# First attention of a two-attention transformer kernel: row maxima as undivided products, and the next head's projections, the transposes and the values in other steps

## Reference

```python
H, HD, D = (16, 64, 128)
Q = (x @ Wq.T + bq).reshape(B, N, H, HD)
K = (x @ Wk.T + bk).reshape(B, N, H, HD)
V = (x @ Wv.T + bv).reshape(B, N, H, HD)
scores = jnp.einsum('bnhd,bmhd->bhnm', Q, K)
scores = scores * (SCALE * adaptive_scale)[None, :, None, None] / TEMP
w = jax.nn.softmax(scores, axis=-1)
attn = jnp.einsum('bhnm,bmhd->bnhd', w, V).reshape(B, N, H * HD)
y = x + (attn @ Wo.T + bo)
```

## Time and profile before

| what | value |
| --- | --- |
| median of 3 runs | 2270.84 us (2270.72 to 2274.38) |
| profiled execution, its own time | 2273.7 us |
| span of its profile, first to last instruction | 2271.9 us |
| mean granted TensorE clock | 0.977 of full speed |
| TensorE products busy | 2148.1 us |
| VectorE busy | 1465.8 us |
| ScalarE busy | 1428.5 us |
| GpSimd busy | 1326.7 us |

### The profile page before, as it was taken

The page is one execution under the profiler, slowest core; times in us unless marked ns, Lnnn a source line. Parts: engine busy times, 40 slices in busy tenths (PEclk is TensorE's granted clock), DMA queues, the critical chain, the costliest instruction groups (busy, mean ns, idle before and its releaser), DMA issues.

```text
span 2271.9 us, 50924 instructions
## 1 busy us (share of the span) xinstructions
PE 2148.1 (95%) x21413; PEld 1609.9 (71%) x21413; DVE 1465.8 (65%) x2764; ACT 1428.5 (63%) x1839; POOL 1326.7 (58%) x730
## 2 busy tenths in 40 slices
PE   4999999999999999999999998779999999999998
PEld 3667667667667667667667666557888888878886
DVE  6666666666666666666666665666666666666652
ACT  2677777777777777777777787325554554545553
POOL 4688888788788788788888898122122231221200
PEclk7899999999999999999999999879999999999999
DMA  6211211211211211211211200100000000000000
GB/s 162 57 29 30 57 30 29 58 29 30 57 29 29 57 30 29 57 30 29 57 30 30 57 2 2 47 0 1 1 1 1 1 1 1 1 1 1 1 1 19
DMA packets 46036, 63.33 MB, mean 28 GB/s; under 512 B 9328, under 2 KB 20592, under 8 KB 45552
## 3 DMA queue, kind: packets, MB, share of 16 engines
q1 hardware_dynamic: 45808, 60.08, 11.2%
HBM read 8.67 MB, written 1.05 MB: 4 GB/s over the span
## 4 chain that ended last, share of the span: by engine, by line
PE 83%; DVE 9%; POOL 4%; issue 2%; ACT 1%; SPq 1%; DMA 1%; POOLq 0%; ACTq 0%; DVEq 0%
PE ST L1248 11%; PE ST L1249 9%; PE OO L1191 7%; PE OO L1382 7%; PE RING L1132 5%; PE OO L1192 5%; PE OO L1194 5%; POOL PAB L474 3%; PE OO L1132 3%; PE RING L1335 3%; PE ST L1405 3%; PE ST L1382 3%; PE ST L1409 2%; PE ST L1407 2%; PE RING L1315 2%; PE RING L1119 2%
## 5 line engine op out<-in xcount | busy, mean ns | idle before, releaser
L474 POOL TENSOR_TENSOR PAB<-PR,PAB 128x1024 f16<-128x1024 f32 x512 | 1092.0, 2138 | 228.3 <-ACT PAB L614 205.2
L612 ACT ACTIVATE PR<-ST 128x1024 f32<-128x1024 f32 x512 | 524.7, 1025 | 357.8 <-PE ST L1249 350.6
L826 DVE TENSOR_REDUCE maxes<-RING 128x1 f32<-128x512 f32 x652 | 434.1, 684 | 234.5 <-PE RING L1132 131.6
L614 ACT ACTIVATE PAB<-ST 128x1024 f16<-128x1024 f32 x512 | 521.3, 1018 | 0.0
L1191 PEld LDWEIGHTS OO<-VP,PAB 128*128 128x128 f16 x4096 | 372.5, 96 | 158.1 <-issue 143.5
L1191 PE MATMUL OO<-VP,PAB 128*128 128x66 f16 x4096 | 444.7, 194 | 17.9 <-DVE SHARED L859 13.8
L1248 PE MATMUL ST<-QL,KH 128*128 128x512 f32 x1024 | 448.0, 438 | 0.0
L1192 PE MATMUL OO<-VP,PAB 128*128 128x64 f16 x4096 | 440.7, 194 | 0.0
L1194 PE MATMUL OO<-VP,PAB 128*128 128x66 f16 x4096 | 438.3, 192 | 0.0
L1249 PE MATMUL ST<-QH,KL 128*128 128x512 f32 x1024 | 404.1, 395 | 0.0
L1192 PEld LDWEIGHTS OO<-VP,PAB 128*128 128x128 f16 x4096 | 377.1, 97 | 20.3 <-issue 19.5
(11 more groups left out here) (165 smaller groups left out, 3337.7 us busy)
## 6 DMA issues: line engine op xcount, KB each, us to landing
KH<-HS SPq DMA_DIRECT2D x128, 128.0 KB, 2.3
QL<-HS SPq DMA_DIRECT2D x64, 128.0 KB, 2.4
QL<-F SPq DMA_DIRECT2D x64, 128.0 KB, 2.4
QH<-HS SPq DMA_DIRECT2D x64, 128.0 KB, 2.4
KL<-F SPq DMA_DIRECT2D x64, 128.0 KB, 2.4
X<-in_L_attn_a_x SPq DMA_DIRECT2D x4, 256.0 KB, 3.7
SHARED<-in_rope_cos SPq DMA_DIRECT2D x1, 1024.0 KB, 4.8
SHARED<-in_rope_sin SPq DMA_DIRECT2D x1, 1024.0 KB, 6.9
```

The source lines that it names most:

```text
L474: pool.tensor_tensor(PB[:, s, :], PR[:, step % 2, :], PA[:, s, :], ALU.subtract).then_inc(p_low_ready, 1)
L612: act.activation(PR[:, step % 2, :], ST[step % 2][:, :], ACT.Exp)
L614: act.activation(PA[:, step % SLOTS_A, :], ST[step % 2][:, :], ACT.Exp).then_inc(sa.exps, 1)
L826: dve.reduce_max(maxes[:, i // BLOCKS, i % BLOCKS:i % BLOCKS + 1], bank[:, :], X_AXIS).then_inc(sa.ring_taken, 1)
```

## The change

Each maxima product is now one product over all 128 partitions, QL with KH, where it was a product over 64 partitions: of the first half (QL) for even items and of the second half (QH) for odd ones. Its result has the low part of the queries in it as well. The projections and values of the next head stand in steps 3 and 7 instead of 1 and 4. The transposes stand in step 4 instead of 3; the output product stays in step 5. The lines behind L1132 move up by two.

```diff
-HEAD_STEPS = (1, 4)
+HEAD_STEPS = (3, 7)
...
     if ((ul - 1) % UNITS_A) // BLOCKS == 1 and not (first and ul == 0):
-        items += [("turned",)] if step == 3 else [("output",)] if step == 5 else []
+        items += [("turned",)] if step == 4 else [("output",)] if step == 5 else []
...
                 qt, c = divmod(i, BLOCKS)
                 at = qb * BLK + qt * P
-                row, high = (0, QL) if c % 2 == 0 else (DA, QH)
-                pe.matmul(RING3[item % 3][:, :], high[head % 2][row:row + DA, at:at + P],
-                          KH[head % 2][row:row + DA, c * BLK:(c + 1) * BLK], start=True, stop=True
-                          ).then_inc(sa.ring_put, 1)
+                pe.matmul(RING3[item % 3][:, :], QL[head % 2][:, at:at + P], KH[head % 2][:, c * BLK:(c + 1) * BLK],
+                          start=True, stop=True).then_inc(sa.ring_put, 1)
```

## The result

The changed kernel takes 2237.6 us, the median of five runs (2236.71 to 2238.41), against 2270.72 us for the kernel before on the same chip (2269.56 to 2274.38 over five runs). The ratio is 0.9851 with a 95% interval of 0.9838 to 0.9865: 33.1 us faster, where 33.5 were forecast.

What follows compares the result with a forecast made beforehand. TensorE, busy 95% of the span, was taken to bound the kernel. Gains of 27.4, 15.5 and 1.0 less 10.4 gave 33.5 us, from 2270.84 to 2237 us; own range 2230 to 2246, set range 2226 to 2257.

Steps and rivals of the forecast that it cites:

- (a): First attention's maxima: two full-height products replace each pair, saving 0.055 us in 498 pairs, 27.4 us.
- the gaps stay: Rival: gaps around the maxima come with the ring's banks, so undividing gains nothing; time 2265, chance 0.07.
- a second stream: Rival: undividing leaves both gaps and adds a stream of 0.23 us a pair; time 2380, chance 0.04.
- (b): Projections moved to steps 3 and 7: PV's waits for VectorE in step 2 go, 15.5 us, plus 1.0 in the first block.
- the 29 waits: PV waiting in step 2 for VectorE's product into A2 after a projection: 29 x (2.80 - 2.265) = 15.5 us gained.
- the term for the first block: Very first block: moving a projection out of the low-clock time gains 1.0 us.
- a projection leaves the low clock: Very first block: the projection's two passes, 2.07 us there, take half at twice the clock; 1.0 us gained.
- (c): Transposes moved to step 4, output still in step 5: VectorE's copy stays hidden with 0.9 us to spare, no cost.
- (d): Values moved in block 2: GpSimd's rest delays PV by 0.55 us in 15 heads, 0.26 in 8; 10.4 us lost.
- GpSimd becomes the pace: Rival: GpSimd needs 2.24 us a step beside a working VectorE, reducing the gain to 15; time 2256, chance 0.12.
- does not grow: Step 6: the row product's wait for VectorE's end of the maxima would not grow, first maximum ready 0.1 us earlier.
- 2.50 for step 6: Step 6 of block 2, with its row product, was taken as 2.50 us long, losing some 0.07.

Runs made afterwards that it cites:

- the moves with the earlier rest: Kernel before with projections, values and transposes moved, maxima still divided, and values taken one step sooner on ScalarE and GpSimd: 2258.45 us, ratio 0.9933.
- the change with the earlier rest: Changed kernel with the items of the values taken one step sooner on ScalarE and GpSimd: 2227.1 us, ratio 0.9802 to the kernel before.
- the moves alone: Changed kernel with the half-height maxima products of before, so only projections, values and transposes are moved: 2268.91 us, ratio 0.9985 to the kernel before.
- the third experiment: Changed kernel with GpSimd's rest of the values, and ScalarE's part, taken one step sooner: 2227.1 us against 2272.68 for the kernel before.
- the first experiment: Kernel before with undivided maxima and no other part of the change: 2243.47 us against 2272.68, ratio 0.9872.
- the second experiment: Changed kernel with divided maxima, only the steps of projections, values and transposes moved: 2268.91 us against 2272.68 for the kernel before.
- the version with both edits: Changed kernel with values taken one step sooner on ScalarE and GpSimd, and without L831: 2219.27 us, ratio 0.976 to the kernel before.

## Why the prediction was right, point by point

**(a) Undivided maxima: right.** The pair was priced at 0.52 and two undivided products at 0.46, by the gaps behind score products. After, the gaps are 0.24, 0.22 and 0.24, and a step is 2.21. The nearest measurement is between the moves with the earlier rest and the change with the earlier rest, where no PV waits for the rest of the values: 1304.6 - 1276.1 = 28.5 us beside 27.4. It is not free of the meeting: L831 takes 0.17 in nearly all steps 6 of the first and 0.27 to 0.29 in half of those of the second. The two rivals on this step fall: "the gaps stay" (they closed) and "a second stream" (it came, 0.22 in the kernel after, but the 0.29 that went from the gaps is more). The doubled speed that this last rival rests on did not carry over to a single pair among full-height products: both products together take 0.46 undivided and 0.52 divided. The prediction also read the gaps of 0.33 and 0.43 as the cost of changing the mode. They are not shown to be that, since the gap between two half-height products in turn, 0.34, is as long as the two at the change of height.

**(b) Projections in steps 3 and 7: the price of the 29 waits right, the term for the first block not.** Kernel before to the moves with the earlier rest is 1320.3 - 1304.6 = 15.7, beside 15.5. All 29 waits went. The first block was priced at 1.0; it takes 20.2 instead of 22.7 from its first score product to block 1, 2.5 less, of which 1.0 is lost because the loop starts that much later (63.55 instead of 62.54; the start of the first maxima varies by 1.9 us among the profiles here, and what they wait for is a DMA). TensorE's clock rises to its higher level sooner. The window from 65 to 70 us in the kernel after, to be read beside 0.50 of full speed (1.2 GHz of 2.4) in the earlier trace rows:

```profile
65.00:70.00 5.00, 4.23 (x23) 2.90 (x22) 3.64 (x6) 4.08 (x5) 2.49 (x2) 0.94 0.00 0
```

But the projections don't bring this. With the undivided maxima alone they stand in step 1 as before, and the window shows 1.00 and the block takes 18.7, the shortest of all. In the moves with the earlier rest they stand in steps 3 and 7, and the window shows 0.50 and the block takes 22.9. Over all kernels here this block lasts 18.7 to 20.2 in the five with undivided maxima and 20.5 to 24.6 in the five with half-height ones. So the step of the prediction that failed here is "a projection leaves the low clock": as far as these runs show, what was gained goes with the form of the maxima, whose pairs at the low level the prediction counted as nothing. Why the clock rises earlier with them stays open. The size is uncertain, since the two groups are only 0.3 apart: the moves alone and the moves with the earlier rest have the same work in this block and take 21.4 and 22.9, 1.5 apart.

**(c) Transposes in step 4: right.** Nothing waits ahead of the output products, and with the transposes back in step 3 the time is the same within 2 us.

**(d) The rest of the values: right in kind, place and size.** 0.55 was forecast for block 3's step 3, 0.56 came, in 15 heads; 0.26 for step 7 of block 2 in even heads, 0.20 came. Together 10.4 were forecast, and 10.0 is what the third experiment gets back in these two places. The rival "GpSimd becomes the pace" falls: its mean is 2141 ns, and normal steps are 2.21.

**The sum.** From before to change by these three kernels it is 28.5 + 15.7 - 11.3 = 32.9 us in the loop, and 1.5 ahead of it, beside the forecast 33.5. That the whole comes within half a microsecond has luck in it, as the next part shows.

**What was missed.** The prediction said of step 6 only that its wait for VectorE's end of the maxima "does not grow", from the time at which the maxima are ready. Two things happen there, and neither was in the sum. With undivided maxima the wait shrinks: step 6 comes down by up to 0.20 and not by 0.055, 2.6 us more in all (the first experiment). And in the change L831 meets GpSimd's work. The prediction looked at what VectorE waits for and not at what GpSimd does meanwhile. L831 in the kernel before, over the first attention (count, ns least/median/most), and then in the kernel after:

```profile
L831 DVE TENSOR_SCALAR negparts<-negmax x64: 170/170/283, 59.6 to 1386.5; 128x4 fp32r<-128x4 f32 x64
```

```profile
L831 DVE TENSOR_SCALAR negparts<-negmax x64: 170/274/897, 60.9 to 1351.8; 128x4 fp32r<-128x4 f32 x64
```

In an even head's block 2 of the kernel after, it looks so (VectorE, GpSimd, TensorE):

```profile
284.56 0.29 DVE L831 TENSOR_SCALAR negparts<-negmax 128x4 fp32r<-128x4 f32 x1
284.78 1.13 POOL L466 TENSOR_TENSOR VP<-VF,VP 128x512 f16<-128x512 f32 x1
285.00 0.27 PE L1138 MATMUL RING<-ident,negparts 128*4 128x128 f32 x1
```

L831 now starts at the tail of a subtraction and is held for 0.1, and ends 0.07 after the rest has started; with divided maxima L831 came 0.04 behind the start of the rest (the second experiment). In the kernel after, 40 of the 64 are held: 33 take 0.27 to 0.56 at the tail of a subtraction, and 7 take 0.88 to 0.90, in block 2 of the odd heads, behind the output product, where most of it is hidden. With the undivided maxima alone the steps 6 of blocks 0 and 1 (without output product) take 2.39; in the change, with L831 at 0.27 to 0.29, they take 2.49 to 2.51. Over all the steps 6 the change has 3.9 us more than the undivided maxima alone. That these 3.9 are the price of the meeting is read from the traces, not tested apart: in the even heads' blocks 1 to 3 and the odd heads' block 0 each step 6 is longer by 0.09 to 0.12, and L831 in it by 0.10 to 0.12. In block 2 of the odd heads the step is longer by 0.07.

So the prediction's 2.50 for step 6 was met, but not for its reason: the maxima gave more than it said, and the meeting took it back. The undivided maxima alone give 29.2 and the moves alone 3.8, and that this adds up to the 33.1 of both is chance: the moves alone pay 7.4 for the meeting and 4.9 for (d), the change about 3.9 and 10.0. The forecast had no term for the meeting, and for the moves alone it would have been some 7 us too fast.

**Open.** In even heads step 6 of block 2 takes 2.60 against 2.50 in blocks 0 and 1, though L831 is held there no longer than in those (in block 3, with 2.59, it is: 0.36). The first maximum starts 0.12 behind the row product there and 0.03 elsewhere; it is the next head's first and has more semaphore waits ahead of it. In the version with both edits the same maxima start 0.03 behind a row product that comes at 1.01 instead of 1.18, so such waits, if they are the cause, cost only behind a row product that is itself late. Not tested apart.

## What to carry to other kernels

Price a product by the distance between starts in a row of its own form, and a change of form among products by both distances around it: a pair that shares the array may lose in the gaps around it more than it saves inside. When work of one engine is moved, list the small operations on the other engines' critical paths that it comes to lie beside, since one of 0.17 us can last as long as its neighbour. And ask behind which long step a delayed operation would be free: one step sooner was worth 10 us here.

## What the runs showed of the hardware that was not expected

VectorE's L831, 128x4 numbers, lasted until the GpSimd operation under way when it started had ended: 0.17 free, 0.27 to 0.56 at the tail of a subtraction, 0.61, 0.90 and 1.10 beside the rest of the values (1.12). A start before GpSimd's left it at 0.17: in the kernel before it starts at 271.66 and a subtraction at 271.78. The reduction L830 never showed this: in the kernel after it took 0.17 all 64 times, 40 of them inside an operation of GpSimd.

Two half-height products cost 0.52 together when they use different halves, 0.755 when both use one half (0.52 + 0.235), and 0.46 as two undivided products.
